# Attention of a Perceiver block: scores turned so that no weight needs a transpose, and most values taken in plain f32

## The reference, cut to what matters

```python
q, k = rms_norm(x @ wq) + rope, rms_norm(ctx @ wk_ctx)      # own keys: rms_norm(x @ wk) + rope
scores = q @ concat(k_ctx, k_self).T / sqrt(128)            # 16 x 256 x 4352, own part causal
out = softmax(scores) @ concat(v_ctx, v_self)               # 16 x 256 x 128
x = x + concat_heads(out) @ wo
```

## Time and profile before

| | us |
|---|---|
| median of 3 runs | 1041.6 (1041.54 to 1041.72) |
| profiled execution, span | 1040.1 |
| PE busy | 1034.4 |
| DVE, ACT, POOL busy | 780.6, 610.6, 182.9 |
| attention, first score product to first output product | 234.4 to 734.9 |

### The profile page before, as it was taken

The page is one execution under the profiler, slowest core; times in us unless marked ns, Lnnn a source line. Parts: engine busy times, 40 slices in busy tenths (PEclk is TensorE's granted clock), DMA queues, the critical chain, the costliest instruction groups (busy, mean ns, idle before and its releaser), DMA issues.

```text
span 1040.1 us, 15687 instructions
## 1 busy us (share of the span) xinstructions
PE 1034.4 (99%) x5837; PEld 890.9 (86%) x5837; DVE 780.6 (75%) x1674; ACT 610.6 (59%) x1106; POOL 182.9 (18%) x200
## 2 busy tenths in 40 slices
PE   9999999999999999999999999999999999999998
PEld 8888888888888888888888888889887988888887
DVE  6856777649777777777877777877669977777775
ACT  5434343335765566665556665569469566666664
POOL 4544434330000000000000000002201132222221
PEclk9999999999999999999999999999999999999999
DMA  7758675399004130042200431004540476555540
GB/s 278 231 183 292 205 243 187 130 317 317 11 1 163 56 127 1 2 172 82 92 1 1 172 122 56 1 1 184 202 163 1 152 295 224 191 184 191 192 162 21
DMA packets 64299, 145.76 MB, mean 140 GB/s; under 512 B 3904, under 2 KB 42720, under 8 KB 62688
## 3 DMA queue, kind: packets, MB, share of 16 engines
q1 hardware_dynamic: 64224, 144.77, 40.2%
HBM read 108.55 MB, written 36.21 MB: 139 GB/s over the span
## 4 chain that ended last, share of the span: by engine, by line
PE 97%; DVE 2%; ACT 1%; DMA 1%; issue 0%; SPq 0%
PE bank L511 17%; PE bank L577 17%; PE bank L493 12%; PE bank L616 12%; PE bank L593 11%; PE bank L877 9%; PE bank L618 6%; PE bank L879 4%; PE bank L673 2%; PE bank L686 1%; PE bank L520 1%; DVE scores L1033 1%; PE bank L741 1%; DMA w_ctx_raw<-in_w_ctx 1%; PE bank L847 1%; PE bank L545 0%
## 5 line engine op out<-in xcount | busy, mean ns | idle before, releaser
L1114 DVE TENSOR_TENSOR pT<-bank,pT 128x512 fp32r<-128x512 f32 x272 | 184.8, 689 | 101.8 <-ACT pT L1574 100.0
L1574 ACT CAST pT<-bank 128x512 fp32r<-128x512 f32 x272 | 156.0, 593 | 141.9 <-PE bank L593 138.8
L616 PE MATMUL bank<-pT,vN 128*128 128x512 f32 (+1 forms) x544 | 225.7, 422 | 0.0
L577 PE MATMUL bank<-kT,qT_hi 128*128 128x512 f32 (+2 forms) x576 | 214.4, 391 | 0.7 <-DVE scores L1033 0.7
L1033 DVE TENSOR_SCALAR_CACHE_REDUCE scores<-bank 128x512 f32<-128x512 f32 x256 | 172.6, 686 | 1.6
L593 PE MATMUL bank<-ident,scores 128*128 128x128 f32 x1072 | 161.3, 272 | 0.1
L1545 ACT ACTIVATE scores<-scores,neg_max 128x1024 f32<-128x1024 f32 (+2 forms) x128 | 154.0, 1204 | 6.2 <-DVE neg_max L1045 6.2
L618 PE MATMUL bank<-pT,vN 128*128 128x256 f32 (+1 forms) x544 | 152.5, 280 | 0.0
L511 PE MATMUL bank<-w_ctx_hi,ctx_hl 128*128 128x512 f32 x512 | 144.5, 394 | 0.4 <-ACT w_ctx_hi L1511 0.4
L877 PE MATMUL bank<-fT_parts,e_hl 128*128 128x512 f32 x392 | 139.9, 394 | 0.0
L593 PEld LDWEIGHTS bank<-ident,scores 128*128 128x128 f32 x1072 | 127.1, 140 | 11.5 <-DVE pT L1114 0.6
(11 more groups left out here) (236 smaller groups left out, 1598.4 us busy)
## 6 DMA issues: line engine op xcount, KB each, us to landing
e_raw<-in_experts SPq DMA_DIRECT2D x51, 768.0 KB, 4.4
k_spill<-k_stage SPq DMA_DIRECT2D x16, 1024.0 KB, 5.6
v_spill<-v_stage SPq DMA_DIRECT2D x16, 1024.0 KB, 8.2
vN<-v_spill SPq DMA_DIRECT2D x16, 1024.0 KB, 5.5
kT<-k_spill SPq DMA_DIRECT2D x15, 1024.0 KB, 5.5
ctx_raw<-in_ctx SPq DMA_DIRECT2D x15, 512.0 KB, 4.0
w_raw<-in_w_qkv SPq DMA_DIRECT2D x6, 1024.0 KB, 5.0
wo_sb<-in_wo SPq DMA_DIRECT2D x4, 1024.0 KB, 7.7
```

What stands on the lines that cost most here:

```text
L577: done = e.matmul(bank[b][:, 0:n], qT[a][:, h, qt * P:(qt + 1) * P], kT[:, w, lo:lo + n], start=m == 0, stop=m == 2)
L616: e.matmul(halves[:, :, q0:L], vN[:, 0, kt, :], ring[:, :, i * L + q0:(i + 1) * L], start=kt == 0, stop=False)
L1114: e.tensor_tensor(ring[:, 1, :], bank[tb][:, :], ring[:, 0, :], ALU.subtract).then_inc(p_lo, 1)
L1574: e.copy(ring[:, 0, :], bank[tb][:, :]).then_inc(p_hi, 1)
```

## The change

- **Scores turned.** 128 keys are now the weights that PE holds, and the 256 queries move (`score`). A group of 256 keys is one bank of 2 x 256 columns, six products of 256 columns. Keys lie on the partitions, as the values need it, and the transposes are gone.
- **Maximum.** It now runs over partitions. ACT copies each group into `s_buf` (`take_scores`), DVE keeps a running maximum over the groups (`running_max`), folds the halves, PE turns it (`turn_max`), DVE reduces it (`reduce_rows`), PE spreads it over all partitions (`spread_max`), DVE subtracts it, 1024 columns at a time (`subtract_max`), and ACT's exponential has no bias.
- **Sum.** POOL adds up the weights of all groups, 512 columns at a time (`add_weights`), and PE multiplies the sum by ones (`sum_weights`).
- **Values.** 12 of 17 groups are multiplied in plain f32, straight from `s_buf`; groups 1, 4, 7, 10, 13 are split as before, with 256 moving columns, the low part of the weights by DVE (1, 7, 13) or POOL (4, 10). Low values are made, spilled and loaded for these five only (`vL`).
- **Order.** One loop of 16 x 17 + LEAD steps, LEAD = 29: step s has the scores of group s and the values of group n = s - 29. DVE subtracts for n + 6, ACT takes exponentials for n + 4 and high parts for n + 2.
- **Output projection.** For the first half of the tokens it is set among the values of the last head from n = 253 (`project_out`). ACT and DVE split `wo` from n = 250; DVE now makes all 16 low parts. The loads of `w_xa`, `w_z` also wait for `sum_all`.

```diff
-NPAIR = KTILES // 2
-LAG = 3
+NG = KTILES // 2
+LEAD = NG + 12
+SUB_AHEAD, EXP_AHEAD, SPLIT_AHEAD = 6, 4, 2
+SCORE_BANKS = (0, 2, 6, 7)
+SPLIT = {1: "dve", 4: "pool", 7: "dve", 10: "pool", 13: "dve"}
+WO_STEP, WO_PRODUCTS = 250, 253
...
 # PE: score(s)
-                for m, (a, w) in enumerate(PRODUCTS):
-                    done = e.matmul(bank[b][:, 0:n], qT[a][:, h, qt * P:(qt + 1) * P], kT[:, w, lo:lo + n], start=m == 0, stop=m == 2)
+                for i in range(2):
+                    dst = bank[b][:, i * L:i * L + L - q0]
+                    for m, (a, w) in enumerate(PRODUCTS):
+                        done = e.matmul(dst, kT[:, w, kt * P:(kt + 1) * P], qT[a][:, h, q0:L], start=m == 0, stop=m == 2)
...
-            def turn_weights(h, kk):
-                    done = e.transpose(bank[tb][:, i * P:(i + 1) * P], s_buf[2 * z + qt][:, kt * P:(kt + 1) * P], ident[:, :])
 # PE: weigh(n)
-                    e.matmul(halves[:, :, q0:L], vN[:, 0, kt, :], ring[:, :, i * L + q0:(i + 1) * L], start=kt == 0, stop=False)
-                    done = e.matmul(halves[:, 0, q0:L], vN[:, 1, kt, :], ring[:, 0, i * L + q0:(i + 1) * L], start=False, stop=kt == KTILES - 2)
+                    if g in SPLIT:
+                        e.matmul(dst[:, 0:L], vN[:, kt, :], ring[:, 0, cols], start=kt == 0, stop=False)
+                        e.matmul(dst[:, 0:L], vN[:, kt, :], ring[:, 1, cols], start=False, stop=False)
+                        done = e.matmul(dst[:, 0:L], v_lo_part[:, i, :], ring[:, 0, cols], start=False, stop=False)
+                    else:
+                        done = e.matmul(dst[:, q0:L], vN[:, kt, :].bitcast(F32), weights[:, cols], start=kt == 0, stop=kt == KTILES - 1)
...
 # PE: the loop
+            for s in range(NH * NG + LEAD):
+                if s == BEFORE_TURN:
+                    turn(NT - 1)
+                n = s - LEAD
+                in_turns(score(s), weigh(n), n)
+                h, k = divmod(s - NG, NG)
+                if h in range(NH):
+                    if k == 2:
+                        turn_max(h)
+                    if k == 5:
+                        spread_max(h)
+                h, k = divmod(n - NG, NG)
+                if k == 0 and h in range(H15):
+                    sum_weights(h)
+                if WO_PRODUCTS <= n < WO_PRODUCTS + H15:
+                    project_out(0, n - WO_PRODUCTS)
+            sum_weights(H15)
+            for h in range(5):
+                project_out(1, h)
+            project_out(0, H15)
...
 # DVE
+                    dve.wait_ge(maxed, plan.maxed[s - 1])
+                    e.tensor_tensor(run_max[:, :], src[:, :], run_max[:, :], ALU.max).then_inc(maxed, 1)
+                    rows = quad(h, j).rearrange("p g (t q) -> p (g t) q", t=2)
+                    e.tensor_tensor(rows, rows, top.unsqueeze(1).to_broadcast([P, 4, L]), ALU.subtract).then_inc(subbed, 1)
...
+            for s in range(NH * NG + LEAD):
+                n = s - LEAD
+                running_max(s)
+                for h, j in quads_at(n + SUB_AHEAD):
+                    subtract_max(h, j)
+                if n + SPLIT_AHEAD in plan.lo["dve"]:
+                    rest_of_weights(n + SPLIT_AHEAD)
+                if WO_STEP < n <= WO_STEP + NH:
+                    rest_of_wo(n - WO_STEP - 1)
...
 # ACT
+                e.copy(s_buf[h % 2][:, g, :], bank[SCORE_BANKS[s % len(SCORE_BANKS)]][:, :]).then_inc(taken, 1)
+                e.activation(quad(h, j), quad(h, j), ACT.Exp, scale=SCALE).then_inc(expd, 1)
+                e.copy(ring_of(n)[:, 0], weights_of(n)).then_inc(p_hi, 1)
...
 # POOL: add_weights(n)
+                pool.wait_ge(expd, NQUAD * h + g // 2 + 1)
+                elif g < SELF:
+                    pool.wait_ge(summed, SUMS * h + g - 1)
+                    e.tensor_tensor(run_sum[:, :], run_sum[:, :], here, ALU.add).then_inc(summed, 1)
+                else:
+                    for k, (to, lo, w) in enumerate(((0, 0, L), (P, L, P))):
+                        pool.wait_ge(summed, SUMS * h + g - 1 + k)
+                        e.tensor_tensor(run_sum[:, to:to + w], run_sum[:, to:to + w], here[:, lo:lo + w], ALU.add).then_inc(summed, 1)
+                    e.tensor_tensor(both_sum[:, :], run_sum[:, 0:L], run_sum[:, L:2 * L], ALU.add).then_inc(summed, 1)
...
 # SP
-            sp.wait_ge(pv, NH * NPAIR)
+            sp.wait_ge(pv, NH * NG)
+            sp.wait_ge(sum_all, NH)
             e.dma_start(w_xa[:, :, :], t["w_in"][:, :, DI:2 * DI]).then_inc(w_xa_in, 16)
```

More of the change, by code:

```diff
@@ L106, in __init__ @@
     def __init__(self):
-        self.chunks = []
-        self.number = {}
-        self.in_step = {}
-        self.spread_bank = {}
-        self.bank_history = {b: [] for b in range(8)}
-        self.parts, self.part_number = [], {}
-        self.parts_in_step, self.parts_at_end = {}, {}
-        self.turn = 0
-        waiting = []
-        self.ring = (0, 2, 6, 7, 4, 3) + 2 * (0, 1, 2, 6, 7, 4, 3) + 8 * (0, 1, 2, 6)
-        for c in EARLY_CHUNKS:
-            self.add(0, 0, c)
-        self.first = list(range(len(self.chunks)))
@@ L173, in before @@
[L173 to L193 removed]
+        self.groups, self.number = [], {}
@@ L196, in seen, with split_before, lows, width @@
+        self.split = [n for n in range(NH * NG) if n % NG in SPLIT]
+        self.lo = {e: [n for n in self.split if SPLIT[n % NG] == e] for e in ("pool", "dve")}
+    def split_before(self, n):
+        return sum(1 for m in self.split if m < n)
+    def lows(self, n):
+        e = SPLIT[n % NG]
+        return e, sum(1 for m in self.lo[e] if m <= n)
+def width(g):
+    return GW if g < SELF else L + P
 def seen(kt, qt):
     return qt == 1 or kt < KTILES - 1
+def summed_at(h, g):
+    return SUMS * h + max(g, 1) + (1 if g == SELF else 0)
@@ L200, in heads, with split_tiles, quads_at, subs @@
+def split_tiles(i):
+    return sum(1 for t in range(i) if t // BT in SPLIT)
+def quads_at(n):
+    return [(h, j) for h in range(NH) for j in range(NQUAD) if NG * h + min(2 * j, NG - 2) == n]
+def subs(h, j):
+    return (NQUAD + 1) * h + (j + 1 if j < NQUAD - 1 else NQUAD + 1)
 def heads(ap):
@@ L620, in weigh @@
                         done.then_inc(pv, 1)
                     yield
-            def in_turns(scores, values):
-                products = [score(s) for s in scores]
-                issued = 0
-                for k in range(4):
-                    while issued < (k + 1) * 3 * len(scores) // 4:
-                        next(products[issued // 3])
-                        issued += 1
-                    if values is not None:
-                        next(values)
-                for p in products:
-                    for _ in p:
-                        pass
-                if values is not None:
-                    for _ in values:
-                        pass
@@ new lines, in sum_weights, with project_out @@
+            def sum_weights(h):
+                pe.wait_ge(summed, SUMS * (h + 1))
+                e.matmul(bank[VALUE_BANKS[h % 2]][:, L:2 * L], ones[:, :], both_sum[:, :], start=True, stop=True).then_inc(sum_all, 1)
+            def project_out(tt, h):
+                pe.wait_ge(wo_lo_done, h + 1)
+                pe.wait_ge(oT_lo, h + 1)
+                if h == 0:
+                    if tt == 0:
+                        wait_score_bank_at_end(pe, 0)
+                    else:
+                        pe.wait_ge(ho, 2 * NH - 2)
+                for m, (a, w) in enumerate([(0, wo_hi), (0, wo_lo), (1, wo_hi)]):
+                    done = e.matmul(bank[tt][:, :], outT[a][:, h, tt * P:(tt + 1) * P], w[:, h, :],
+                                    start=h == 0 and m == 0, stop=h == NH - 1 and m == 2)
+                if h == NH - 1:
+                    done.then_inc(wo_done, 1)
@@ new lines, in act_program @@
+            for s in range(NH * NG + LEAD):
+                if s == BEFORE_TURN:
+                    main_of_k(NT - 1)
+                if s == BEFORE_TURN + 2:
+                    last_keys()
+                n = s - LEAD
+                if n + SPLIT_AHEAD in plan.split:
+                    high_of_weights(n + SPLIT_AHEAD)
+                take_scores(s)
+                for h, j in quads_at(n + EXP_AHEAD):
+                    exponential(h, j)
+                h, k = divmod(n - NG, NG)
+                if k == 2 and h in range(H15):
+                    finish_head(h)
+                if WO_STEP <= n < WO_STEP + NH:
+                    main_of_wo(n - WO_STEP)
@@ L2000, in sp_program @@
-            sp.wait_ge(pv, NH * NPAIR)
+            for s in range(NH * NG):
+                h, g = plan.groups[s]
+                group, last = h // REP + 1, h % REP == REP - 1 and h < H15
+                if last and (g % 4 == 3 or g == SELF):
+                    sp.wait_ge(scored, s + 1)
+                    if group == 1:
+                        wait_spilled(k_out, g // 4)
+                    load_k(group, g // 4)
+                n = s - LEAD
+                if n >= 0:
```

(4 more changed lines are left out.)

664 lines of the change are left out of this document (310 added, 354 removed).

## The result

The changed kernel takes 1142.71 us (median; 1142.25 to 1144.23) against 1041.66 on the same chip: 1.097 times the time before, 95% interval 1.0955 to 1.0986. The forecast was 1021.0 us, with 1000 to 1045 as its range. The profiled execution has a span of 1140.5 us, 100.4 more than before.

The account below looks back on a forecast made before the run. PE bounded the kernel before; after, PE, DVE and POOL lie at 28.1 to 28.4 us a head. 234.4 + 21.2 + 4.2 + 413 + 51 + 13.3 = 737.1, 20.6 us less: 1021.0 us, range 1000 to 1045.

Parts of the forecast that it names:

- I add 0.5 us for this, a choice: 28.9 us a head: Attention: allowance for PE, DVE and POOL drifting against each other, 0.5 us on 28.4, giving 28.9 us a head.
- The halfway rival: Attention: POOL's gap 0.12 to 0.2, or DVE late at group 13; 29.7 to 30.5 us a head, 1033 to 1045; chance 0.22.
- Nine short ones ... 3.7: DVE per head: mask, fold, reduce, reciprocal, product and the like at 0.3 to 0.55 us each, 3.7 us.
- a hold of 0.4: DVE per head: each of six instructions with two SBUF inputs waits some 0.4 us for POOL, 2.4 us together.
- 24 x 0.08 = 1.9: PE per head: change from f32 to f32r behind 24 plain products, 0.08 us each, 1.9 us.
- I take half, 0.43: PE per head: a 256-column plain f32 product takes half of a 512-column one, 0.43 us; 10.1 us for 12 groups.
- 1.27: POOL per head: each of 15 additions of 512 columns takes 1.27 us.
- The rival of POOL's own chain: Attention: a gap of 0.24 between dependent additions makes POOL need 30.7 to 31 us a head, 1051 to 1055; chance 0.14.
- POOL busy over 90%: Sign to look for: POOL busy over 90% of the attention.
- The lead and its stall: Start of attention: 29 groups of scores alone, 21.2 us, then PE stalls 4.2 us for group 1's low part, done at 261.5.
- The tail: End of attention: 29 groups of values without scores; POOL ends 51 us after step 272 and the last head's sum waits.
- PE waiting for both_sum, some 10 us: Sign to look for at the end of the attention: PE waits some 10 us for POOL's both_sum.

Follow-up runs that it names:

- the reordered kernel: Changed kernel, five splits kept, low parts asked for a step earlier and the end of a head taken nine steps later: 1043.0 us, ratio 0.9997.
- the run above: Changed kernel with five splits, low parts a step earlier, end of a head nine steps later, POOL's additions cut to one column: 997.2 us.
- the best kernel: Changed kernel with no group split and the end of a head taken nine steps later: 1012.8 us, ratio 0.9723.
- seven steps later: Changed kernel with the end of a head (reciprocal, product, copy, low part) taken seven steps later: 1139.1 us; without splits, own maxima from the bank: 1052.0.

## Why the prediction was wrong

**The step that failed** is "I add 0.5 us for this, a choice: 28.9 us a head", the price of three engines waiting for each other. In its place stand 7.0 us a head in which PE waits for DVE (6.7 for the low parts and 0.3 for L1090) and 2.9 us more of busy time than the 26.8 that PE needs, at the low clock: together the 36.7. The work of the engines was close: DVE 29.3 busy for 28.2 forecast. And 28.9 is near what this work can give, since the reordered kernel makes it in 29.2. But three engines at 28 us each meet that only if every result is ready in the order in which it is wanted.

The half us was set without laying DVE's instructions of a head out in program order. Done from the trace: PE starts on group 1 at 411.93 and wants group 7's low part six steps later, at 421.3. DVE starts on the same step at 414.08, since it waits for ACT's copy of the scores, and has 11.5 us of work in it and the next four, the low part included. That ends at 425.6, 4.3 us late. At the forecast's own prices the same list is some 9.3 us, and 2 us late (an estimate from these rows); so the order alone could be read beforehand, the full size could not.

What is shown: of the 7.8 us a head over the forecast, 7.5 go with the order (29.2 for 36.7), with the same instructions. In these are the 2.3 that filling the stall gave back, the clock's fall, which hangs on the wait. But the order isn't the cause by itself. With the order as it was, 6.3 go with POOL's additions and 2.8 with the reciprocal: the wait needs both, a burst longer than it was priced and a low part behind it, and taking either away gives back a good part of it. The halfway rival named DVE's lateness, but at group 13 (1.08 and 1.10 us in the trace) and for 0.8 to 1.6 us a head.

**DVE's terms.** "Nine short ones ... 3.7" was too small: the nine are 0.55, 0.48, 0.41, 1.75, 0.42, 1.39, 1.24, 0.41 and 0.28 = 6.9 us. Of the 3.2 us between, 1.2 had been added apart as a hold of 0.4 for three of them; 2.0 are missing, for the reciprocal, taken like the others, is 1.75, and the hold of the two maxima of the own tokens is 0.96. The low parts are 1.44 each for 1.09. Together DVE's 35 instructions of a head last 31.2 us, 3.0 over the forecast. That its busy time came out only 1.1 us over is luck: instructions in a row overlap (one of 0.68 us starts at 416.81 and the next at 417.41, 0.60 apart), which the forecast didn't count, and that makes good 1.9.

**PE's terms.** 28.4 forecast, 26.8 by the run above. The excess is the change of format, "24 x 0.08 = 1.9". Steps of a plain group at full clock:

```profile
404.74 0.59 PE L597 MATMUL bank<-qT_hi,kT 128*128 128x256 f32 x2
405.16 0.28 PE L597 MATMUL bank<-qT_lo,kT 128*128 128x256 f32 x1
405.29 0.59 PE L627 MATMUL bank<-weights,vN 128*128 128x256 f32 x2
405.53 0.59 PE L597 MATMUL bank<-qT_hi,kT 128*128 128x256 f32 x2
```

From 404.74 to 405.53 are three f32r products and one plain f32 (two records): 0.79 us. Less 3 x 0.118 this leaves 0.436 for the f32 product, the change included. "I take half, 0.43" was right, and nothing comes on top. By the same row a split group saves 0.16 us (1.42 for 1.58), 0.8 a head, and 0.8 was measured.

**POOL.** "1.27" was right (the median is 1.284), and the gap nearly: most of those between 300 and 440 us are 0.08, the others up to 0.15. Here are five additions in 6.93 us, 0.13 apart on average:

```profile
418.11 6.93 POOL L1864 TENSOR_TENSOR run_sum<-run_sum,weights 128x512 f32<-128x512 f32 x5
429.36 1.27 POOL L1877 TENSOR_TENSOR pT<-weights,pT 128x512 fp32r<-128x512 f32 x1 [4.32 <-ACT pT L1587]
```

The rival of POOL's own chain, on the right side of 1041.6, is not what happened (it asked for a gap over 0.22): POOL idled 4.3 us a head here, for a high part that ACT could not make until PE went on. "POOL busy over 90%" was false (49% of the span, 67% of a head).

**The region.** The lead and its stall: the low part of group 1 was done at 266.2 us for 261.5, +4.7. From there to the last score product (784.9, step 272 at 785.2): 519.0 for 411.3, +107.7, which is 7.5 for each of the 14.3 heads. The tail: 51.8 for 51. The last sum product to the first product of w_z (837.0 to 857.9): 20.9 for 13.3, +7.6. Together 120.8 us, and the forecast missed by 121.7. The tail's length was right, but "PE waiting for both_sum, some 10 us" was not: it was 0.26 us, with 8.2 us for low parts of the weights and 3.1 for those of wo in its place, and POOL's additions held by DVE's low parts of wo (six in 10.28 us, 1.71 each). The 7.6 us are mostly a queue that I didn't look at:

```profile
846.81 4.63 DVE L1160 TENSOR_TENSOR w_xa_lo<-w_xa,wx_hi 128x1024 fp32r<-128x1024 f32 x4 [4.09 <-ACT wx_hi L1624]
851.36 0.68 DVE L1164 TENSOR_TENSOR x_sb<-x_sb,bank 128x512 f32<-128x512 f32 x1
...
853.84 0.55 DVE L965 TENSOR_SCALAR un<-x_sb,moments,rstd 128x512 f32<-128x512 f32 x1 [0.67 <-POOL rstd L1817]
```
```profile
854.45 1.12 PE L511 MATMUL bank<-ident,un 128*128 128x128 f32 x4 [5.90 <-DVE un L965]
```

DVE's x_sb of the first tokens stands behind the four low parts of w_xa, whose load starts only once the last sum is taken. The forecast asked this of w_z and not of w_xa, issued ahead of it. The products behind the wait of 5.90 us start at a granted clock of 0.50 (854 to 858 us). A wait of 5.75 us for the same instruction is left in the best kernel too; moving L1164 ahead of L1160 wasn't tried.

**The rules of the Trainium skill.** TensorE: Matmul & The Clock Gate (Back-to-back issue gap) gives the gap of an isolated product, and going by it a head's f32r products would have cost 1.2 us less (an estimate from its table). It doesn't hold for this stream: f32r products stand 0.12 us apart after the change as before it (starts at 403.79, 403.91, 404.03 and 404.15 us behind the wait for group 13 shown above). No run here has isolated products. SBUF — State Buffer (Who interferes with whom), the shared read interface of two-input DVE work and GpSimd, is borne out in kind: with the additions cut, and with one input in PSUM, the hold is gone. For short instructions the hold is 0.96 us of POOL's 1.28, nearer to the page's full hold than to the 0.4 us I took.

## What to carry to other kernels

When several engines end up at equal load, sum the work and then write one period of each in program order: for each result that another engine waits for, find the last point at which both engines were level, and count the work of each from there. Here DVE had 2.2 us of delay and 11.5 of work where PE had six steps, 9.4 us, and two changes of order were worth 100 us with the same instructions. Look first at bursts: the mean load says nothing of them, and a price that is 2 us too low for a head can stand in one of them whole. An operation that is moved is given to a place where the engine idled in the trace, behind whatever is awaited there: seven steps later gained 3.7 us with the splits and was part of a loss of 20 without them, nine gained 19. Price the saving of a split against its helpers: 0.16 us of PE for each group, for 0.6 us of ACT and 0.7 to 1.8 of DVE or 1.3 of POOL. And take a period from steady heads alone: here the last two are shorter by 6 to 7 us.

## What the runs showed of the hardware

- The reciprocal of 128x256 f32 on DVE takes 1.75 us; a copy of the same shape from the same bank 0.41, a product 0.42.
- A DVE instruction with both inputs in SBUF is often held beside POOL's additions, a short one as long as a wide one: in the changed kernel 256 columns took 1.39 us for 0.43, 128 columns 1.24 for 0.29, 512 columns up to 1.77 for 0.68 (1.44 on average). Not each is held: the fold took 0.48 for 0.42 there, and with the end of a head seven steps later the 256 columns took 0.42. With one input in PSUM the two maxima were not held; with nothing split the hold then passed to the fold (1.26 for 0.42), with five splits it did not.
- Behind 4.3 us in which PE had nothing to do the granted clock fell to 0.50 for nearly 7 us; behind the waits of about 1 us, and one of 2.12 us, it stayed at 1.00; behind one of 2.53 us it fell to 0.50 as well. Filling the gap with products of no use kept it at 1.00 and gave 2.3 us a head.
- f32r products of 256 columns stand 0.118 us apart, each with its own load of weights, and a plain f32 product of 256 columns set between them takes 0.436 us in all, with nothing visible on top for the change of format.
